# Message layer of a four-layer graph network: tail panels sent by SP from the edge stage, rows normalised in groups of four blocks, root table loaded early, node vector on ScalarE

## What is computed

```python
def _layernorm(x, axis=-1, eps=1e-05):
    m = jnp.mean(x, axis=axis, keepdims=True)
    v = jnp.var(x, axis=axis, keepdims=True)
    return (x - m) / jnp.sqrt(v + eps)

def _L2_gnn_ref(mu, x, edge_index, edge_w, W1, W2, W3, W4):   # x is node_vec1
    h_x = relu(x @ W1.T)
    h_e = relu(edge_w[:, None] @ W2.T)
    h_mu = relu(mu @ W3.T)
    dst, src = edge_index[1], edge_index[0]
    cat_feat = jnp.concatenate([h_x[dst], h_e, h_mu[dst]], axis=1)
    agg = jax.ops.segment_sum(cat_feat, src, num_segments=n_nodes)
    agg = relu(agg @ W4.T)
    return relu(h_x + h_mu + agg)

x = _layernorm(x + _L0_gnn_ref(...))            # graph convolution
x = _layernorm(x + _L1_gnn_ref(...))            # edge network
x = _layernorm(x + _L2_gnn_ref(x, node_vec1, edge_index, edge_weight, ...))  # message layer
x = _layernorm(x + _L3_gnn_ref(x, ...))         # polynomial of degree 10
```

## Time and profile before

| | |
|---|---|
| median of 3 runs | 1686.84 us (1685.07 to 1688.77) |
| profiled execution | 1688.62 us, its span 1686.8 us, mean granted clock 0.932 |
| busy: TensorE matmul / VectorE / ScalarE / GpSimd | 1439.1 (85%) / 1261.0 (75%) / 616.2 (37%) / 44.5 us (3%) |
| a row load of the edge stage | 640.0 KB, then 728.0, 84.5 and 19.5 KB |
| a panel | 684.2 KB and 79.4 KB (112 and 13 rows of 6256 bytes) |
| node vector, two rows | 24.4 KB |

### The profile page before, as it was taken

The page is one execution under the profiler, slowest core; times in us unless marked ns, Lnnn a source line. Parts: engine busy times, 40 slices in busy tenths (PEclk is TensorE's granted clock), DMA queues, the critical chain, the costliest instruction groups (busy, mean ns, idle before and its releaser), DMA issues. The chain is left out here.

```text
span 1686.8 us, 45445 instructions
## 1 busy us (share of the span) xinstructions
PE 1439.1 (85%) x16795; PEld 1326.9 (79%) x16795; DVE 1261.0 (75%) x3685; ACT 616.2 (37%) x1161; POOL 44.5 (3%) x64
## 2 busy tenths in 40 slices
PE   0745459978996999999999859599999999999993
PEld 0534357768995888888888739599999999999993
DVE  5999878874436888888888757668678687676785
ACT  0269859990103777777777610100000000000000
POOL 1100000000000000000000030000000000000000
PEclk9977869997998999999999969699999999999996
DMA  1000025440003454544232060000000000000000
GB/s 21 7 0 0 0 76 150 140 144 26 2 1 101 131 154 120 152 120 133 84 95 87 21 168 2 6 2 2 3 2 2 3 2 2 3 2 3 2 2 21
DMA packets 36998, 83.95 MB, mean 50 GB/s; under 512 B 22927, under 2 KB 23943, under 8 KB 36849
## 3 DMA queue, kind: packets, MB, share of 16 engines
q1 hardware_dynamic: 32216, 74.42, 15.3%
q10 hardware_dynamic: 4410, 7.43, 1.9%
q0 software_dynamic: 224, 0.13, 0.0%
HBM read 60.76 MB, written 21.14 MB: 49 GB/s over the span
## 5 line engine op out<-in xcount | busy, mean ns | idle before, releaser
L1742 PE MATMUL L_psA<-L_parts,mat 125*128 125x192 bf16 x6250 | 517.2, 246 | 0.0
L1742 PEld LDWEIGHTS L_psA<-L_parts,mat 125*128 125x128 bf16 x6250 | 515.5, 98 | 1.1 <-DVE L_parts L1820 1.0
L1176 PEld LDWEIGHTS L_ps_pre<-L_drow,mat 128*128 128x128 bf16 x2250 | 128.4, 98 | 30.3 <-issue 1.1
L1684 ACT COPY L_wk<-L_Wk 128x64 f32 (+1 forms) x10 | 2.0, 243 | 404.3 <-PE L_psA L1742 404.3
L1807 DVE TENSOR_REDUCE L_sumr<-L_psA 125x64 f32<-125x192 f32 x250 | 89.5, 358 | 76.8 <-PE L_psA L1742 75.8
L1176 PE MATMUL L_ps_pre<-L_drow,mat 128*128 128x32 bf16 (+3 forms) x2250 | 132.7, 212 | 0.0
L643 DVE TENSOR_TENSOR onehot<-iota_bf,codes 128x1024 bf16<-128x1024 bf16 x150 | 98.8, 688 | 29.3 <-PE ps_extra L706 22.5
L774 PE MATMUL L_psA<-L_gparts,mat 125*128 125x192 bf16 x1250 | 112.3, 252 | 4.4 <-DVE L_gparts L787 4.4
L1365 DVE TENSOR_TENSOR L_e<-L_e,mat 128x512 f32<-128x512 f32 x125 | 86.3, 690 | 39.4 <-ACT L_e L1263 39.4
L774 PEld LDWEIGHTS L_psA<-L_gparts,mat 125*128 125x128 bf16 x1250 | 108.5, 102 | 5.3 <-DVE L_gparts L787 4.7
L1199 PE MATMUL L_ps_agg<-L_hot,mat 128*128 128x125 bf16 x1500 | 103.5, 219 | 3.8 <-DVE mat L1370 3.8
(11 more groups left out here) (297 smaller groups left out, 2530.7 us busy)
## 6 DMA issues: line engine op xcount, KB each, us to landing
L_drow<-rows_d SPq DMA_DIRECT2D x25, 728.0 KB
m_d<-panel SPq DMA_DIRECT2D x25, 684.2 KB
mat<-rows_d SPq DMA_DIRECT2D x25, 640.0 KB, 4.2
mat<-m_d SPq DMA_DIRECT2D x16, 684.2 KB
mat<-m_d ACTq DMA_DIRECT2D x9, 684.2 KB
L_drow<-rows_d SPq DMA_DIRECT2D x25, 84.5 KB
m_d<-panel SPq DMA_DIRECT2D x25, 79.4 KB
mat<-m_d SPq DMA_DIRECT2D x16, 79.4 KB
```

What stands on the lines that cost most here:

```text
L1176: last = nc.tensor.matmul(ps_pre[bank][:, to:to + n], w, drow[k][:, of:of + n], start=False, stop=(r == 2 and cc == pieces[-1][0]))
L1742: last = nc.tensor.matmul(ps[:, 0:3 * D], t.mat[0:B, kb, b * B:b * B + P], parts[src][:, kb].rearrange("p r d -> p (r d)"), start=(kb == 0 ...
```

## The change

1. The tail panels are no longer sent by ScalarE at the start of the message layer. SP sends them at the end of its list in the edge stage: three when the last first-layer product is done, six when `node2` of the last block is done.
2. The edge stage ends without `normalize`. The first 24 `bn_aggr` stand ahead of the last `keep_out`, the 25th follows it. The subtraction and the multiplication move into the message layer, by groups of four blocks (`scale_rows`), with the root on ScalarE as the first step there; TensorE turns a group once it is scaled (`x2_set`). The statistics lie in `t.src1` from the edge stage on.
3. ScalarE's last instruction of the edge stage is a root of one element, in place of the root of all.
4. The parts of the node vector are made by ScalarE (`node_values`), after a wait for the vector behind the first copy. GpSimd has no part in it any more.
5. Two of VectorE's steps on `mix` move to the first block of the edge stage; `turn(1)` stands ahead of the weight products.

```diff
 def kept_norm_buffers(t):   # new; edge_network and message_layer take bn, mv, std, rstd from it
+    old = lambda lo, hi: t.src1[0:B, lo * NB:hi * NB].rearrange("p (b s) -> p b s", s=hi - lo)
+    return old(0, 6), old(6, 8), t.src1[0:B, 8 * NB:9 * NB], t.src1[0:B, 9 * NB:10 * NB]
...
 edge_network, first block, vector:
                 S(nc.vector.tensor_tensor(t.xb[:], t.xb[:], nb2[:].unsqueeze(1).broadcast_to([B, NB, D]), ALU.add))
+                dve.wait_ge(mix_clear, 1)
+                S(nc.vector.tensor_copy(l2.mix[0:D, D:2 * D], c.ident[0:D, 0:D]))
                 dve.wait_ge(wd_set, 1)
...
+                dve.wait_ge(l2.w_in, 16 * 7)
+                S(nc.vector.tensor_scalar(l2.mix[D:D + 2, D:2 * D], l2.mix[D:D + 2, D:2 * D], c.sign[D:D + 2, :], 0.0,
+                                          ALU.mult, ALU.max))
...
 edge_network, second block, sync:
                 sp.wait_ge(panels_in, 32 * HEAD)
+                def tail_panel(i):
+                    for to, of in spans(t.mat[:, i, :], m2_d[i]):
+                        sp.dma_start(to, of).then_inc(l2.tail_in, 16)
+                sp.wait_ge(pre_done, NG * NB + 1)
+                for i in range(HEAD, HEAD + 3):
+                    tail_panel(i)
+                sp.wait_ge(p_ready, NB + 1)
+                sp.wait_ge(out_ready, NB + 1)
+                for i in range(HEAD + 3, NB):
+                    tail_panel(i)
...
 scalar:
-                roots(nc, act, c, mv, std, var, root)
+                nc.scalar.activation(std[0:1, 0:1], c.eps[0:1, :], ACT.Sqrt)
...
 vector:
+                dve.wait_ge(stats, NB - 1)
+                for b in range(NB - 1):
+                    nc.vector.bn_aggr(mv[:, b, :], bn[:, b, :])
                 keep_out(NB - 1, 0)
-                dve.wait_ge(out_kept, NB + 1)
-                dve.wait_ge(stats, NB - 1)
-                S.n = 3 * (NB + 1)
-                normalize(nc, dve, S, t.xa, bn, mv, std, rstd, t.xb, var, root, NB - 1)
+                take_stats(NB - 1)
+                dve.wait_ge(stats, NB)
+                nc.vector.bn_aggr(mv[:, NB - 1, :], bn[:, NB - 1, :])
...
 message_layer, gpsimd:
                 nc.gpsimd.memset(feat[D:P], 0.0).then_inc(feat_clear, 1)
-                pool.wait_ge(nv_in, 16)
-                for g in range(len(groups)):
-                    nv = feat[D:D + 2, cols(g)]
-                    nc.gpsimd.tensor_scalar(nv, nv, c.sign[D:D + 2, :], 0.0, ALU.mult, ALU.max).then_inc(nv_set, 1)
...
 scalar:
-                for b in range(HEAD, NB):
-                    for to, of in spans(t.mat[:, b, :], m2_d[b]):
-                        act.dma_start(to, of).then_inc(tail_in, 16)
+                nc.scalar.activation(std[:], mv[:, :, 1], ACT.Sqrt, bias=c.eps[0:B, :]).then_inc(x2_root, 1)
...
+                def node_values(g):
+                    nv = feat[D:D + 2, cols(g)]
+                    nc.scalar.activation(nv, nv, ACT.Relu, scale=c.sign[D:D + 2, :]).then_inc(nv_set, 1)
                 keep_columns(0)
+                act.wait_ge(nv_in, 16)
                 for g, blocks in enumerate(groups):
+                    node_values(g)
                     if g + 1 < len(groups):
                         keep_columns(g + 1)
...
 tensor:
                 def turn(g):
+                    pe.wait_ge(x2_set, g + 1)
...
                 turn(0)
-                pe.wait_ge(w_in, 16 * 7)
+                turn(1)
...
-                pe.wait_ge(tail_in, 32 * (NB - HEAD))
+                pe.wait_ge(l2.tail_in, 32 * (NB - HEAD))
...
 vector:
-                dve.wait_ge(w_in, 16 * 7)
+                def scale_rows(g):
+                    blocks = slice(groups[g][0], groups[g][-1] + 1)
+                    some = [B, len(groups[g]), D]
+                    S(v.tensor_tensor(t.xa[:, blocks], t.xa[:, blocks], mv[:, blocks, 0:1].broadcast_to(some),
+                                      ALU.subtract))
+                    if g == 0:
+                        dve.wait_ge(x2_root, 1)
+                        S(v.reciprocal(rstd[:], std[:]))
+                    S.wait()
+                    v.tensor_tensor(t.xb[:, blocks], t.xa[:, blocks], rstd[:, blocks].unsqueeze(2).broadcast_to(some),
+                                    ALU.mult).then_inc(x2_set, 1)
+                scale_rows(0)
+                scale_rows(1)
...
+                for g in range(2, len(groups)):
+                    scale_rows(g)
+                S(v.reduce_sum(we[:], t.wsum[:, :, 0:6].rearrange("p b (s r) -> p b s r", r=3), X))
                 dve.wait_ge(g_ps, 1)
```

More of the change, by code:

```diff
@@ L828, in norm_buffers, with kept_norm_buffers @@
             sb("rstd", [B, NB], F32))
+def kept_norm_buffers(t):
+    old = lambda lo, hi: t.src1[0:B, lo * NB:hi * NB].rearrange("p (b s) -> p b s", s=hi - lo)
+    return old(0, 6), old(6, 8), t.src1[0:B, 8 * NB:9 * NB], t.src1[0:B, 9 * NB:10 * NB]
 def gcn_layers(nc, a, c, t, l0, l1):
@@ L1018, in edge_network @@
         z1 = sb("z1", [H, B], F32)
-        bn, mv, std, rstd = norm_buffers(sb)
+        bn, mv, std, rstd = kept_norm_buffers(t)
         ps_pre, ps_z2, ps_agg = ([pb(f"{n}{i}") for i in range(2)] for n in ("ps_pre", "ps_z2", "ps_agg"))
@@ L1114, in _ @@
                                                 ).then_inc(q_done, 1)
+                dve.wait_ge(l2.w_in, 16 * 7)
+                S(nc.vector.tensor_scalar(l2.mix[D:D + 2, D:2 * D], l2.mix[D:D + 2, D:2 * D], c.sign[D:D + 2, :], 0.0,
+                                          ALU.mult, ALU.max))
         (panels_in, rows_hot, staged, pre_done, e1_ready, z2_done, biased, silu2_done,
-         cut, mid_done, split_done, hot_ready, seg_done, agg_ready, n1_ready, z1_ready, out_ready, out_kept, stats, xs_ready, p_ps, p_ready, var,
-         root, step) = map(sem, (
+         cut, mid_done, split_done, hot_ready, seg_done, agg_ready, n1_ready, z1_ready, out_ready, out_kept, stats, xs_ready, p_ps, p_ready,
+         step) = map(sem, (
              "panels_in", "rows_hot", "codes_staged", "pre_done", "e1_ready", "z2_done", "biased", "silu2_done",
              "high_cut", "mid_done", "split_done", "onehots_ready", "seg_done", "agg_ready", "n1_ready", "z1_ready", "out_ready", "out_kept", "stats_taken",
-             "xs_ready", "p_product", "p_ready", "var_ready", "std_ready", "net_step"))
+             "xs_ready", "p_product", "p_ready", "net_step"))
         first = lambda b: isinstance(b, int) and b == 0
@@ L1431, in l2_weights @@
     w.mix = sb("mix", [P, 2 * D], F32)
-    w.w_in = ctx.enter_context(nc.semaphore("L2_weights_in"))
+    w.w_in, w.tail_in = (ctx.enter_context(nc.semaphore(n)) for n in ("L2_weights_in", "L2_tail_in"))
     return w
@@ L1455, in message_layer @@
         feat = sb("feat", [P, V], F32)
-        mix, W3T, W4a, W4b, w1c, w2c, w_in = l2.mix, l2.W3T, l2.W4a, l2.W4b, l2.w1c, l2.w2c, l2.w_in
+        mix, W3T, W4a, W4b, w1c, w2c = l2.mix, l2.W3T, l2.W4a, l2.W4b, l2.w1c, l2.w2c
         w1pm, w2pm, ge = sb("w1pm", [D, D + 2], F32), sb("w2pm", [D, 2, B], F32), sb("ge", [B, 2, D], F32)
@@ L1460, in message_layer @@
         rest = t.src1[0:B, 10 * NB:10 * NB + 4 * D].rearrange("p (b d) -> p b d", d=D)
-        old = lambda lo, hi: t.src1[0:B, lo * NB:hi * NB].rearrange("p (b s) -> p b s", s=hi - lo)
-        bn, mv = old(0, 6), old(6, 8)
-        std, rstd = t.src1[0:B, 8 * NB:9 * NB], t.src1[0:B, 9 * NB:10 * NB]
+        bn, mv, std, rstd = kept_norm_buffers(t)
         psT, psM, psZ = ([pb(f"{n}{i}") for i in range(2)] for n in ("psT", "psM", "psZ"))
         psG = pb("psG")
-        (feat_clear, zeroed, nv_in, tail_in, turned, x2t, hmu_ps, hmut, z_ps, parts_ready, nv_set, w_set, g_ps, g_set, sums,
+        (feat_clear, zeroed, nv_in, x2_root, x2_set, turned, x2t, hmu_ps, hmut, z_ps, parts_ready, nv_set, w_set, g_ps, g_set, sums,
          kept, var, root, step) = map(sem, (
-             "feat_clear", "zeroed", "nv_in", "tail_in", "x2_turned", "x2T_ready", "hmu_product", "hmuT_ready", "z_product",
+             "feat_clear", "zeroed", "nv_in", "x2_root", "x2_set", "x2_turned", "x2T_ready", "hmu_product", "hmuT_ready", "z_product",
              "parts_ready", "nv_set", "w_parts", "g_product", "g_set", "sums_ready", "rows_kept", "var_ready",
@@ L1536, in hidden @@
                                      ).then_inc(hmu_ps, 1)
-                turn(1)
                 pe.wait_ge(zeroed, 2)
@@ L1566, in _ @@
                 v = nc.vector
-                dve.wait_ge(w_in, 16 * 7)
+                def scale_rows(g):
[11 more added lines that the diff above has]
+                scale_rows(1)
                 S(v.memset(w1pm[:, 0:D], 0.0))
-                S(v.tensor_copy(mix[0:D, D:2 * D], c.ident[0:D, 0:D]))
                 S(v.tensor_scalar(w1pm[:, D:D + 1], w1c[:], 0.0, None, ALU.max))
@@ L1573, in _ @@
                 S(v.tensor_scalar(w2pm[:, 1, :], c.ones[0:D, 0:B], w2c[:], -1.0, ALU.mult, ALU.mult))
-                S(v.tensor_scalar(mix[D:D + 2, D:2 * D], mix[D:D + 2, D:2 * D], c.sign[D:D + 2, :], 0.0, ALU.mult,
```

(5 more changed lines are left out.)

## The result

The changed kernel takes 1692.57 us (median of 10 runs), the one before 1687.65 us (10 runs): the ratio of the runs is 1.0027, with a 95% interval of 1.0014 to 1.0040. The change makes the kernel 4.6 us slower by the ratio (2.4 to 6.7 us by its interval), 4.9 us by the medians. The profiled execution of after has a span of 1689.1 us at a mean granted clock of 0.936, against 1686.8 us at 0.932.

What follows compares the result with a forecast made beforehand. Two parallel 32 us lines, panels (ending last) and node work (1.2 us earlier), set the start of the message layer's sums. Terms 3.8 + 0 + 0.3 = +4.1 us on 1686.84 us give 1690.9 us; range 1684.5 to 1694.5.

Steps and rivals of the forecast that it cites:

- The vector lands with the panels: Message layer: on SP's queue the node vector lands behind six panels, at 992.0 (990.0 to 993.5) against 987.6.
- SP's issuing eats the normalising's gain at the border: End of edge stage: SP's twelve issues take 4.8 to 6.0 us, so the message layer opens at 975.2 to 976.4.
- From landing to the hidden product of group 1: Message layer: values and copy on ScalarE take 1.2 us, so this product starts at 993.2, 4.2 us later.
- Clock in the group loop: Message layer's group loop: TensorE runs partly at 1.2 GHz after its idle time, costing 0.7 us (0.2 to 1.4).
- Clock in the sums: Start of the message layer's sums: half speed as before, 0, with -1.9 us if kept, +0.7 us if slower to rise.
- First block of the edge stage: Edge stage's first block: the mix copy and sign step added there cost +0.3 us (0 to 0.5).
- Edge loop: Loop of the edge stage: taken as unchanged, with no term of its own in the sum.
- Root table: Ahead of the root: the table's load is already early, so nothing changes, 0.
- Normalising: Moved into the message layer by groups: all seven ready by 7 us after its opening, hidden by the vector's wait.
- R1: Rival: the vector is served beside the panels, landing at 987.4; 1686.2 us, no change; chance 0.14.
- R2: Rival: the vector passes the panels, landing at 982.4, sums at 1002.2; 1681.1 us, faster; chance 0.08.
- R3: Rival: SP's issuing is slower than counted and the block ends late; 1695 us for an opening at 990; chance 0.06.

Runs made afterwards that it cites:

- e1: The changed kernel with the node vector sent on ScalarE's queue, the panels staying on SP's; ratio to before 1.0007.
- e4: The changed kernel with six panels sent by SP in the message layer and the node vector behind them; ratio to before 1.0029.
- e6: As e4, but with three of the six panels ahead of the node vector and three behind; 1686.35 us, executed once.
- e8: The changed kernel with the two mix steps moved from the edge stage's first block to the end of its loop; 1693.38 us, executed once.
- e3: The changed kernel with six panels sent by SP in the message layer, behind the node vector; 1678.05 us, ratio to before 0.9947.
- e7: e3 with one panel ahead of the clearing wait, mix steps late, weight products and their copies reordered; 1676.90 us, ratio to before 0.9928.
- e2: The changed kernel with all nine panels sent by ScalarE in the message layer again; ratio to before 0.9982.

## Why the prediction was right

The direction, the size (+4.1 us forecast, +4.6 us by the ratio) and the cause hold. That the totals lie so close is in part luck: two terms were too small, and with their measured values the sum would be 4.6 + 0.8 - 0.2 = 5.2 us; the interval of 2.4 to 6.7 us can't tell the two sums apart. Step by step:

- *The vector lands with the panels.* Forecast 992.0 - 970.0 = 22.0 us from node2; the value step starts at 21.8 us. The row loads were read rightly, and e1, e4 and e6 show the order in the queue by itself. By the Trainium skill's page "DMA: Bandwidth & Descriptors", section "Queues, rings and completion order", each transfer engine takes the descriptors of one ring in order and serves several rings in turn, packet by packet. The runs agree: 11.3 us from issue to use behind the panels on one queue (after), 7.9 us beside them on the other (e1).
- *SP's issuing eats the normalising's gain at the border.* Forecast opening 5.2 to 6.4 us from node2, measured 6.9: twelve issues took 6.32 us, 0.53 us each instead of 0.40 to 0.50. As forecast it is hidden, which e4 shows (opening at 1.0 us, sums no earlier).
- *From landing to the hidden product of group 1.* Forecast 1.2 us, measured 1.36: ScalarE's value step takes 0.71 us, not 0.5. The shift is 4.14 us, forecast 4.2.
- *Clock in the group loop.* Mis-sized. Forecast 0.7 us with bounds of 0.2 and 1.4, measured 5.76 - 4.14 = 1.6 us at the second z product. TensorE was at half clock from 991.3, where it resumed, to 997.3, 6.0 us, longer than both rises that I had taken (3.9 and 5.4 us), so the whole first z product, the turn and most of the hidden product behind it ran at 1.2 GHz. The sums start 4.6 us later instead of 3.8.
- *Clock in the sums.* At half speed again, as forecast, for 3.4 instead of 3.85 us. From the start of the sums to the end of VectorE's last multiplication it is 663.9 us against 664.1. One reading behind this term was wrong: of the four pauses in the last layer that I gave as 2.1 us, three are 2.08 to 2.15 us and the third is 2.67 us. The outcome doesn't hang on it.
- *First block of the edge stage.* Forecast +0.3 us, measured +0.8 in the one pair of profiles; e8 leaves open how much of it is the steps.
- *Edge loop.* Taken as unchanged. From VectorE's first step in it to the start of the last node2 it is 432.9 us in after and 432.3 in before, and 431.8 to 433.1 in the eight other kernels, so no difference stands out from the spread.
- *Root table.* Its load starts at 967.37, 0.7 us before node2 ends, as in before (969.28): 0, as forecast.
- *Normalising.* Hidden, as forecast. A pass over 256 values took 0.42 us instead of 0.3, and two of the weight steps took 1.68 and 1.55 us (0.32 and 0.61 in before) and ended at 978.7, right behind GpSimd's clearing (978.6), all under ScalarE's 12.05 us wait. In e3 that cover is gone, and there the order of these steps did cost: with another order z starts at 10.6 us in e7 instead of 12.1, and 0.7 us of that reach the sums.

The rival R1 (served beside the panels) is what two queues do: e1, where the vector does land as R1 has it (17.9 us, R1: 17.4), is at 1.0007 of before, so no change, as R1 priced it, though its sums start at 38.8 us from node2 and R1 had 37.3; R2's price was right in kind, since in e3 a vector that lands early brings 9 us. R3 fell: SP issued twelve transfers in 6.32 us with the panels in flight, and the layer opened at 975.01, far from 985.

## What to carry to other kernels

Before bulk transfers are moved to a queue, list what that queue still has to issue behind them: here a small transfer that many waited for landed when the bulk did, at the bulk's pace (3.05 us a panel). Send the small one first (used after 2.4 us in e3), or on another queue (7.9 us in e1), and then the bulk. And a gain at a block border goes to whoever ends last there, so count the new owner's issuing too.

## What the runs showed of the hardware

- A transfer of 24.4 KB in two rows was used 2.4 us after its issue with nothing ahead (e3), 7.3 to 7.9 us beside panels on the other queue (before, e1, e2), 9.3 us behind three panels (e6) and 15.9 us behind six (e4).
- The rise of the clock after TensorE resumes took 3.4 us at the sums of after and 6.0 us in its group loop. In e3, whose sums start at 995.41 behind the same 2.53 us pause, it took 5.8 us; its profile has 0.50 up to 1000 and 0.71 as the mean of the next two:

```profile
998.00:1000.00 2.00, 2.00 (x15) 1.90 (x14) 0.32 (x1) 0.00 (x0) 0.00 (x0) 0.50 0.00 0
1000.00:1002.00 2.00, 2.00 (x20) 1.95 (x18) 1.05 (x5) 0.00 (x0) 0.00 (x0) 0.71 0.00 0
```

By an estimate from these rows, 2.4 us more at half speed cost 1.2 us, and e3 does need 1.15 us more from the start of its sums to the opening of the next layer (61.09 us, after 59.94). To the end of VectorE's last multiplication it needs 2.7 us more (666.6 us, after 663.9); the other 1.5 us lie in the polynomial layer, and what they are is not shown. Such differences are as large as the gains of the smaller edits here, and so the stage times from node2 were compared beside the totals.
